# Scaling the squared queries on GpSimd instead of ScalarE, and an earlier channel comparison on VectorE, in a seven-stage fused image pipeline

## The reference, cut to what matters

```
x = x + mixture_of_experts_1x1(gn(x))
x = x + depthwise3x3_prune_pointwise_prune(gn(x))   # h is zeroed by channel where max|h| < 4
x = x + attention(gn(x))
x = x + box_filter_3x3(gn(x))
# in attention, per token n (784 tokens, 256 channels):
q2 = q * q;  q2n = q2 / (sum(q2) + 1e-7);  q2n = q2n / max(norm(q2n), 1e-12)
t2 = einsum(q2n, k2n^T v) / sqrt(784)
```

## Time and profile before

| what | us |
|---|---|
| time, median of three runs | 1683.83 (1683.47 to 1685.27) |
| time of the profiled execution | 1683.19 |
| its span, first to last instruction | 1681.4 |
| PE matmul busy | 1543.4 (92%) |
| DVE busy | 1452.5 (86%) |
| ACT busy | 1369.0 (81%) |
| POOL busy | 421.4 (25%) |

### The profile page before, as it was taken

How to read it: one execution, slowest core, us unless ns; L and a number is a source line. 1 busy time by engine, 2 the same in 40 slices (tenths; PEclk the granted TensorE clock), 3 DMA queues, 4 the chain that set the end, 5 groups by cost and what they waited for, 6 DMA issues and landing times. The chain is left out here.

```text
span 1681.4 us, 26750 instructions
## 1 busy us (share of the span) xinstructions
PE 1543.4 (92%) x8190; PEld 1144.9 (68%) x8190; DVE 1452.5 (86%) x2530; ACT 1369.0 (81%) x3496; POOL 421.4 (25%) x269
## 2 busy tenths in 40 slices
PE   3569999999999999999999999999999999998994
PEld 2247777677777767777776777777677777766773
DVE  5867799999989999998999999899999989998646
ACT  3368988888888888888888888888888888878872
POOL 1111212233321223332122333212233321223224
PEclk8689999999999999999999999999999999999997
DMA  4000011100111110011111001111100111000000
GB/s 143 20 20 20 20 39 39 39 20 20 39 38 38 38 38 19 19 38 38 38 38 38 19 19 38 38 38 38 38 19 19 38 38 39 20 20 20 20 20 39
DMA packets 21058, 55.58 MB, mean 33 GB/s; under 512 B 2321, under 2 KB 3345, under 8 KB 21010
## 3 DMA queue, kind: packets, MB, share of 16 engines
q1 hardware_dynamic: 20914, 54.98, 9.3%
q10 hardware_dynamic: 96, 0.00, 0.0%
HBM read 29.29 MB, written 25.69 MB: 33 GB/s over the span
## 5 line engine op out<-in xcount | busy, mean ns | idle before, releaser
L769 DVE SCALAR_TENSOR_TENSOR h<-xpad,dw_sb,h 128x784 f32<-128x784 f32 x512 | 534.3, 1097 | 1.1
L540 PE MATMUL tile_ps<-wqk,xn_parts 128*112 128x512 f32 x1344 | 363.6, 425 | 0.0
L540 PEld LDWEIGHTS tile_ps<-wqk,xn_parts 128*112 128x112 f32 x1344 | 234.6, 175 | 80.2
L1223 POOL TENSOR_SCALAR xpad<-x,gn_r,gn_s 128x784 f32<-128x784 f32 x64 | 64.8, 1020 | 784.1 <-DVE gn_s L700 784.1
L448 PE MATMUL conv_ps<-h,pw_masked 128*128 128x392 f32 x512 | 183.5, 502 | 42.6 <-DVE x L805 37.1
L582 PE MATMUL tile_ps<-k,xT 112*128 112x256 f32 x896 | 205.1, 388 | 7.7 <-ACT xT L1029 7.7
L582 PEld LDWEIGHTS tile_ps<-k,xT 112*128 112x128 f32 x896 | 174.2, 195 | 40.1 <-issue 8.4
L963 ACT ACTIVATE junk<-x 128x784 bf16<-128x784 f32 x192 | 163.1, 851 | 40.6 <-DVE x L805 20.7
L570 PE MATMUL conv_ps<-x,mixed 128*128 128x392 f32 (+1 forms) x512 | 177.4, 499 | 2.2 <-ACT mixed L997 1.1
L448 PEld LDWEIGHTS conv_ps<-h,pw_masked 128*128 128x128 f32 x512 | 93.4, 192 | 111.6 <-DVE x L805 38.7
L448 PE MATMUL conv_ps<-xn_parts,w_out 128*128 128x392 f32 x768 | 153.1, 348 | 0.0
(11 more groups left out here) (143 smaller groups left out, 3020.5 us busy)
## 6 DMA issues: line engine op xcount, KB each, us to landing
x<-x SPq DMA_DIRECT2D x32, 784.0 KB, 4.3
out<-x SPq DMA_DIRECT2D x32, 784.0 KB, 3.5
expert_sb<-expert_rows SPq DMA_DIRECT2D x8, 256.0 KB, 5.5
x<-w_qk SPq DMA_DIRECT2D x1, 512.0 KB
x<-w_vT SPq DMA_DIRECT2D x1, 256.0 KB
x<-w_ln SPq DMA_DIRECT2D x1, 256.0 KB
pw_sb<-pw_wT SPq DMA_DIRECT2D x1, 256.0 KB
gmean<-group_mean SPq DMA_DIRECT2D x1, 64.0 KB, 4.0
```

The costliest lines, as they stand in the source:

```text
L540: mm = nc.tensor.matmul(bank, xn2_parts[:, u, i, m * TOK:(m + 1) * TOK], wqk[:, v, i, :], start=False, stop=(i == J - 1 and u == 1))
L769: ins = nc.vector.scalar_tensor_tensor(acc, view, scalar, acc, ALU.mult, ALU.add)
```

## The change

`scale_q` moves from the end of ACT's step to the end of POOL's step, as seven TENSOR_SCALAR (multiply by the pointer scalar `q_alpha`, add 0.0) with two waits and one `hold`. On DVE `h_mask` is placed ahead of `box_sums` instead of behind it. Everything else stays.

```diff
@@ DVE step
                 if B.active:
                     depthwise(B, slice(1, 3))
+                if C_.active:
+                    h_mask(C_)
                 if F.active:
                     box_sums(F, range(BOX_STEPS))
-                if C_.active:
-                    h_mask(C_)
                 if B.active:
                     depthwise(B, slice(3, 5))
@@ ACT
-            def scale_q(D):
-
-                act.wait_ge(alpha_step.sem, alpha_step.at(D))
-                for m in range(M):
-                    nc.scalar.activation(q2[:, m, :], q2[:, m, :], ACT.Identity,
-                                         scale=q_alpha[:, 2, m:m + 1]).then_inc(qa_ready.sem, 1)
@@ ACT step
                     sum_squares(1, A, x1[:, A.odd], x1_ready)
-                if D.active:
-                    scale_q(D)
@@ POOL
+            def scale_q(D):
+
+                pool.wait_ge(q4_ready.sem, q4_ready.at(D))
+                pool.wait_ge(alpha_step.sem, alpha_step.at(D))
+                hold(pool, "pool")
+                for m in range(M):
+                    nc.gpsimd.tensor_scalar(q2[:, m, :], q2[:, m, :], q_alpha[:, 2, m:m + 1], 0.0, ALU.mult,
+                                            ALU.add).then_inc(qa_ready.sem, 1)
@@ POOL step
                 if C_.active:
                     mask_weights(C_)
+                if D.active:
+                    scale_q(D)
```

## The result

The changed kernel takes 1703.14 us (median of four, 1701.22 to 1703.69) against 1683.65 us (median of four of the kernel before): ratio 1.0114, 95% interval 1.0096 to 1.0131. It is slower by 1.1%, as forecast (1700). The profiled execution took 1701.22 us with a span of 1699.4, 18.0 us over the one before.

What follows compares the result with a forecast made beforehand. The prediction took a loop through DVE and PE as the bound. It added 29 x 0.37 + 28 x 0.26 = 18.0 us, less 1.5 in the drain, to 1683.2, giving 1699.7, forecast as 1700 us, range 1679 to 1711.

Steps and rivals of the forecast that it cites:

- The loop through DVE and PE: Whole step, 49.1 us: lengthening DVE between gate logits and reciprocal lengthens the step one for one.
- The scaling on POOL costs the taps 0.65 us: DVE's last five taps: 3.5 POOL scaling pieces at 0.18 us each lengthen them by 0.65 us a step.
- ACT's relief: Group norm chain: without scaling on ACT, `gn_sd` starts up to 0.39 us earlier, of which PE can use 0.22.
- part 2: Scaling on POOL: the chain to `kx_low` ends 0.65 - 0.39 = 0.26 us later a step, in 28 steps.
- The comparison shut out by POOL's addition: Ahead of DVE's box additions: the comparison waits for POOL's addition, +0.13 us, with 0.07 saved behind the box sums.
- The masking among the additions: POOL's two earlier masking pieces get between DVE's box additions two to four, costing 0.31 us a step.
- parts 3 and 4: Comparison moved ahead and masking thereby earlier: together +0.37 us a step straight onto `make_x3`, in 29 steps.
- No wait for the scaled queries at L465: PE at L465: POOL's scaling ends early enough that PE never waits for the scaled queries.
- The drain: Last steps: one late comparison no longer holds up `make_x3` for 1.6 us, saving 1.5 us in all.
- slots cost nothing: Rival: POOL's short instructions lengthen no tap or box addition and ACT's gain remains; 1677 us, chance 0.15.
- one half of it: Rival: taps shut POOL out but box additions don't; -0.1 to +0.17 us a step, 1680 to 1688, chance 0.23.
- full exclusion: Rival: each POOL piece met costs DVE its whole 0.47 us; 2.26 us a step, 1746 us, chance 0.06.

Runs made afterwards that it cites:

- e1: Kernel before with only DVE's channel comparison moved ahead of the box additions, scaling still on ScalarE: 1692.5 us, ratio 1.0068.
- e2: Kernel before with only the scaling moved to POOL, comparison still behind the box additions: 1690.3 us, ratio 1.0055.
- e10: Kernel before with the scaling split, five token groups on POOL and two on ScalarE, comparison in its old place: 1705.7 us, ratio 1.0138.
- e9: Kernel before with the scaling split, four token groups on POOL and three on ScalarE, comparison in its old place: 1714.3 us, ratio 1.0186.
- e11: e9 plus 20 semaphore increments that nobody waits for, ahead of ScalarE's loop: 1676.6 us, ratio 0.9967 to the kernel before.
- e3: Kernel before with the scaling split, three token groups on POOL and four on ScalarE, comparison in its old place: 1675.9 us, ratio 0.9963.
- e5: e4 plus 30 semaphore increments that nobody waits for, ahead of ScalarE's loop: 1679.6 us, ratio 0.9979 to the kernel before.
- e7: e1 with POOL's masking also made to wait until DVE's four box additions are done: 1686.5 us, ratio 1.0019 to the kernel before.
- e8: Kernel before plus seven POOL fills of a spare tile where the change scales, scaling still on ScalarE: 1684.0 us, ratio 1.0008.
- e4: Kernel before with ScalarE scaling one token group of seven, the other six left out, none on POOL: 1683.2 us, ratio 1.0002.
- e6: Changed kernel plus 40 semaphore increments that nobody waits for, ahead of ScalarE's loop: 1704.5 us, ratio 1.0126 to the kernel before.
- e12: e10 plus 25 semaphore increments that nobody waits for, ahead of ScalarE's loop: 1678.4 us, ratio 0.9981 to the kernel before.

## Why the prediction was right, point by point

- **The loop through DVE and PE**, one for one: right. e1 lengthens the box stretch by 0.32 and the step by 0.30; e2 leaves that stretch alone.
- **The scaling on POOL costs the taps 0.65 us**: 0.66. The term was right by luck, as two errors cancel: not 3.5 pieces at 0.18 (which is 0.63; I wrote 0.65) but three at 0.22, as e10 and the change show; the fourth, though it ends in the taps, is free (e9, e11). The ramp step from which I took 0.18 held one piece at 0.14, whose first part lay in the tap before, and one at 0.22.
- **ACT's relief, 0.39 in the chain**: right (0.41 to 0.03 behind `gn_var`). That PE could use no more than 0.22 of it was too low: e3 and e5 show 0.29 a step, 0.24 in the odd and 0.34 in the even ones. The net of part 2, +0.26, was measured as 0.27; PE's wait at L504 grew to 0.36 and not to 0.5.
- **The comparison shut out by POOL's addition**: right in the profile (1.84 us), wrong in its price: +0.13 - 0.07 forecast, nothing measured (e7). From the start of the first addition before to its end it was 2.66 us, from the start of the comparison to the end of the first addition after it 2.71 (801.67 to 804.38): +0.05, which the 0.07 behind the box sums takes back. The masking among the additions: 0.31 forecast, 0.32 measured. The sum of parts 3 and 4, 0.37, was 0.05 to 0.07 too high, about 2 us over 29 steps.
- **No wait for the scaled queries at L465**: right.
- **The drain**: I gave it -1.5 us; the stretch behind the 20 steps is 2.9 us longer, of which three full steps make 1.8. The saving did not come: the two late comparisons, now ahead of the box additions, are still shut out: they take 1.3 us each, where they took 1.7, and 0.16 alone. Beyond that a single trace cannot price the drain: the three steps that begin at the 33rd L686 take 130.8 us before and 131.9 after, but also 131.9 in e8.
- **A step of 49.7 us**: 49.64, and in the even ones 49.78 on average, some of which is the code fetch that I did not foresee: about 2 us in all.
- **The total** is nearer than its terms: about 2 us too much for parts 3 and 4 stand against about 2 us of fetches and a saving of 1.5 us in the drain that did not come. That they nearly cancel is luck.
- The rival "slots cost nothing" falls by e2, "one half of it" by e1 and e2 together, as each half costs; "full exclusion" falls by the price of 0.22 for a piece of 0.47.
- The rule of the Trainium skill (SBUF — State Buffer, Who interferes with whom) holds for DVE's long instructions: a piece of POOL waits for the tap that runs (1.21 us for 0.47 of work). That a piece of POOL costs DVE its own whole length is more than the taps show (0.22 for 0.47). The comparison of 0.16 us reads a single SBUF tile, of which the rule as I quoted it does not speak, and is shut out to the end of POOL's addition all the same. So is the first tap of a channel half, a TENSOR_SCALAR that also reads a single SBUF tile: in the kernel before it takes 0.62 us for one half and 2.10 for the other, which meets POOL's addition:

```profile
781.61 0.62 DVE L766 TENSOR_SCALAR h<-xpad,dw_sb 128x784 f32<-128x784 f32 x1
...
790.97 2.35 POOL L1234 TENSOR_TENSOR row_sums<-row_sums,x3pad 128x784 f32<-128x784 f32 x1
...
791.64 2.10 DVE L766 TENSOR_SCALAR h<-xpad,dw_sb 128x784 f32<-128x784 f32 x1
```

## What to carry to other kernels

An idle engine is not a free one: here work that goes to POOL was paid by DVE whenever DVE's instruction beside it read SBUF alone, two tiles (taps, additions) or one (comparison, a half's first tap), and not when it read PSUM and one SBUF tile (`make_x1`, `make_x3`). So count how much fits beside the PSUM readers and split there: three or four of seven here gain 0.3 to 0.4% (four only once ScalarE's loop starts at its old place in the code), all seven lose. Making a small input ready earlier is a loss if what it releases then slows an instruction on the path. And before a few per cent are put down to an edit of a looped kernel, compare the packets of the instruction queue and the two halves of an unrolled turn.

## What I had not expected of the hardware

The place of an engine's loop in its code is worth up to 37 us here. The instruction queue of the page, before the change 23 packets, in the changed kernel and in e9:

```profile
q14 instruction: 73, 0.60, 0.1%
```

The 50 more come inside the loop, five for each of ten turns of two steps, 8 KB each, three of the five within 5 us of the turn. With them ScalarE's first instruction of the turn comes 1.6 to 4.3 us later, seen from L686, than that of the odd step. They appeared when ScalarE had 20, 25, 30 or 35 instructions fewer ahead of its loop (e9, e10, e4, the change and e2) and not with 15 fewer (e3) or with the number restored (e5, e6, e11, e12). The Trainium skill (Runtime: NRT & Kernel Launch, Instruction fetch mechanics) says that a taken branch whose target is outside the current window of two pages forces a fetch before execution goes on. The trace agrees with that form. Where the borders of the pages lie, and why e9's one stop lasts 3.9 us where those of e10 (2.3 and 1.3), the change (3.1) and e4 (2.7) are shorter, was not found out. Nor was the price of a stop worked out: e9 loses 4 us a turn, e10 2.6 and e4 only 0.65. In the traces of e4, e9, e10 and the change ScalarE is the only engine whose "issue" waits differ between odd and even steps by more than 0.25 us; that other engines' lists add to it is not excluded.
